# Queries and keys of all batches kept on chip, the forget gates' math in two groups, and half of a batch's rows normalised by the scalar engine

## The chip, the core and the metric

The kernel runs on one core of one Trainium2 chip. The core has a matrix engine (PE; PEld is its weight load), a vector engine (DVE), a scalar engine (ACT), GpSimd (POOL) and a sync engine (SP) that here only issues DMAs and waits. A name with a q (SPq, ACTq, POOLq) is the queue of DMAs that an engine issues. Each engine works through its own list of instructions in order; a semaphore wait holds everything behind it on that engine. The metric is the device time of one execution in microseconds (us).

## The reference

Two layers over x of 16 batches x 256 rows x 256 columns, all in float32:

```python
# layer 1: matrix-LSTM cross attention, queries from LN(x), keys and values from ctx
q = layernorm(x)                                   # (x - mean) / sqrt(var + eps)
i_gate = concat(q, ctx, ctx) @ igate_kernel + igate_bias     # 8 heads
f_gate = concat(q, ctx, ctx) @ fgate_kernel + fgate_bias
cs = cumsum(log_sigmoid(f_gate))                   # along the 256 rows
log_D = where(tril, cs_row - cs_col + i_gate_col, -inf)
m = max(log_D, -1);  D = exp(log_D - m)
C = (q @ k.T / sqrt(32)) * D                       # per head, 32 columns each
h = C / (max(|sum(C)|, exp(-m)) + 1e-6) @ v
x = x + head_layernorm(h) * outnorm_weight
# layer 2: mixture of 8 experts, top 2 per row
xn = layernorm(x)
y = sum over 2 best experts of p_e * w3_e (silu(w12_e xn)[:512] * (w12_e xn)[512:])
out = x + y
```

## The kernel before, in words

The program runs through four stages, one after the other on every engine.

**Stage 1, gates** (helper `gating`, `stage1` on each engine, 16 batches, b = 0 to 15). SP loads x (`X1`, L383) and the transposed context (`CT1`, L391). DVE takes mean and variance (L704, L708) and writes both halves of the normalised rows (`Q1`, L720). ACT turns the variance into 1/sqrt (Ln and Exp, L510, L512). PE's `turn` transposes `Q1` into a PSUM bank (four transposes, L1133); ACT copies that to `QT1` (L531), and SP stores it to the DRAM tensor `qT_scratch` (L386). PE's `gates` multiplies `QT1` and `CT1` by the gate kernels (eight matmuls, L1145 and L1147), ACT copies the 16 x 256 result to `GS1` (L537), SP stores that to `gate_scratch` (L396). The engines run this skewed: in step b of the loop DVE does the statistics of batch b and the rows of b-1; ACT does Ln and Exp of b, the copy of b-1, the gate copy of b-2; PE does `turn(b-1)` and then `gates(b-2)`. In every second step ACT also rounds a piece of the expert weights w12 to a high part (`high`, L517) and POOL subtracts it to get the low part (`low`, L1015); a piece is 128 x 512. w12 has 32 pieces; stage 1 does 8 of them, 8 more go between the stages and before, 16 in stage 2.

**Between the stages.** The gates of all 16 batches x 8 heads are read back as two 128 x 256 tiles (L405). ACT and DVE compute log-sigmoid, the two scans and the running maximum (L559 to L563, L735 to L743), ACT, POOL and DVE split two tiles into three bfloat16 parts (`parts`), ACT makes the decay factors `dcol` (L571 to L573), PE transposes them (L1160), DVE copies them to `cols` (L747). SP stores the parts to `g_scratch` and `negM_scratch` (L433, L435). SP also loads mask constants (L409, L412) and the first queries. Stage 2 waits for all of it.

**Stage 2, mixing** (`mixing`, `step(b, i)`). Per batch SP loads from DRAM the gate rows (`LG`, `RM`), the keys again (`KT`, L417), the queries spread by head (`QBD`, four DMAs, L419), the context with a column of ones (`AUG`, L463), the keys as rows (`KN`, L464) and half of the queries once more (`QTB`, L465). PE computes the exponents (L1177), scores (L1190), products with the values (L1208), the state of the first half of the rows (L1221; its input `VW` is made by POOL, L1054, from `AUG` and `cols`), its product with the queries (L1242) and the router's scores. ACT's Exp (L583) and DVE's product (L799, `combine`) stand between.

**Routing** (DVE: top 2, positions, one-hot tables, `hots`, L941 and L942) with PE's small matmuls; SP loads the eight w3 tensors meanwhile (L479). **Experts**: 71 tiles of 128 rows, gathered by POOL and added back to the output.

Of the kernel before, what the change touches and what calls it, by code (L numbers as in the profile page):

```python
# [34 lines left out]
P = 128  # L35
# [26 lines left out]
MROWS = GROWS + HALF + 1  # L62

# [20 lines left out]
def build(nc, x, ctx, ctxv, ctxT, gkq, gkk, gkv, ibias, fbias, onw, w12T, w3T, gateT, ident, lgc, rmc, trib, iota, iota16, codes, floors, spares, out):  # L84

    qT_dram = nc.dram_tensor("qT_scratch", (B, P, NG, S), F32).ap()
    gate_dram = nc.dram_tensor("gate_scratch", (B, 2 * NH, S), F32).ap()
# [11 lines left out]
    with ExitStack() as stack:  # L99
# [3 lines left out]
        def sem(name):  # L103
# [26 lines left out]
        KT = [sb(f"kt{i}", [P, NG, S], on=early) for i in range(2)]  # L130
# [15 lines left out]
        rs1 = [sb(f"rs1_{i}", [P, NC], on=a) for i in range(4)]  # L146
        parts = sb("parts", [P, 2, PARTS, S], BF16, on=a)
        rest = sb("rest", [P, 2, PARTS - 1, S], on=a)
        zeros = sb("zeros", [P, S], on=a)
        zrow = sb("zrow", [P, ROW], on=a)  # L150

        a1 = ExitStack()
        X1 = [sb(f"x1_{i}", [P, NC, E], on=a1) for i in range(4)]
        CT1 = [sb(f"ct1_{i}", [P, NK, S], on=a1) for i in range(4)]
        a1.close()

        gi, gf, fa, fm, fe, fl, lsg, cs, g, M, negM, mx = (
            sb(n, [P, S], on=a) for n in ("gi", "gf", "fa", "fm", "fe", "fl", "lsg", "cs", "g_", "M_",
                                          "negM", "mx"))
        dcol = sb("dcol", [P, 4, P], on=a)  # L160
        a.close()
# [3 lines left out]
        QTB = [sb(f"qtb{i}", [P, NG, P], on=m) for i in range(2)]  # L165
# [16 lines left out]
        m.close()  # L182
        early.close()
# [43 lines left out]
        def two(name):  # L227
# [6 lines left out]
        qT_out, gate_out = two("qT_out"), two("gate_out")  # L234
# [5 lines left out]
        pair_in, pair_dve, pair_act, m_parts, g_parts, g_there, g_rest, parts_out = sems(  # L240
            "pair_in", "pair_dve", "pair_act", "m_parts", "g_parts", "g_there", "g_rest", "parts_out")
        abs_ready, log_ready, g_ready, dcol_ready, cols_psum, cols_ready = sems(
            "abs_ready", "log_ready", "g_ready", "dcol_ready", "cols_psum", "cols_ready")
        wst_in = two("wst_in")
        pieces2_in = [sem(f"pieces2_in_{n}") for n in range(B // 2 - 2)]
        w_hi, w_lo = sems("w_hi", "w_lo")
# [23 lines left out]

        def gating(eng, step, peeled=4):


            for b in range(peeled):
                step(b, b % 4)
            with eng.Fori(peeled // 4, B // 4) as it:
                for x in range(4):
                    step(it * 4 + x, x)
            for b in range(B, B + 2):
                step(b, b % 4)  # L280
# [33 lines left out]
        def flat(t):  # L314
            return t[:].rearrange("p k s -> p (k s)")

# [3 lines left out]
        PIECES0, PIECES2 = (0, 2), tuple(range(4, B, 2))  # L320
        W0 = len(PIECES0)
        EARLY2 = 2
        W1 = W0 + B
        W2 = W1 + len(PIECES2)

        BUF2 = [flat(t) for t in (Q1[0], Q1[1], QT1[0], QT1[1])] + [t[:] for t in wst]
        IN0, IN1 = 16 * W0 // 2, 16 * (W0 + B // 2) // 2
        K1 = 2 * NC
        LOADS3 = 1 + HG + 3

        LOADSV = 3

        def load2(eng, n):

            at = PIECES2[n] * HID
            eng.dma_start(BUF2[n], w12T[:, at:at + HID]).then_inc(pieces2_in[n], 16)

# [17 lines left out]
        def _(sp):  # L355

            for b in range(2):
                sp.dma_start(X1[b][:], x_t[b]).then_inc(x1_in[b], 16)
            sp.dma_start(id_f[:], ident).then_inc(consts_in, 16)
            for dst, src in ((gq, gkq), (gk, gkk), (gv, gkv)):  # L360
                sp.dma_start(dst[:], src.rearrange("p (k g) -> p k g", k=NK)).then_inc(consts_in, 16)

# [14 lines left out]
            def stage1(b, x):  # L377

                old, o = b - 5, 1 - x % 2
                if has(b, 0) and (not isinstance(b, int) or b >= 2):  # L380

                    wait(sp, q_ready, b - 3)
                    sp.dma_start(X1[x][:], x_t[b]).then_inc(x1_in[x], 16)  # L383
                if has(b, 5):
                    sp.wait_ge(qT_ready, old + 1)
                    sp.dma_start(qT_dram[old], QT1[o][:]).then_inc(qT_out[o], 16)  # L386
                if has(b, 1):

                    y = (x + 3) % 4
                    wait(sp, gates_psum, b - 4)  # L390
                    sp.dma_start(CT1[y][:], ctxT_t[b - 1]).then_inc(ct1_in[y], 16)  # L391
                if isinstance(b, int) and b == 3:
                    later_constants()
                if has(b, 5):
                    sp.wait_ge(gates_ready, old + 1)
                    sp.dma_start(gate_dram[old], GS1[o][:]).then_inc(gate_out[o], 16)  # L396
            gating(sp, stage1, peeled=8)
            for b in range(B + 2, B + 5):
                stage1(b, b % 4)


            for i in range(2):
                sp.wait_ge(gate_out[i], 16 * (B // 2))
            for k, dst in enumerate((gi, gf)):
                sp.dma_start(dst[:], gate_dram[:, k * NH:(k + 1) * NH, :]).then_inc(pair_in, 16)  # L405

            for i in range(2):
# [7 lines left out]
            def load_scores(b, i):  # L415

                sp.dma_start(KT[i][:], ctxT_t[b]).then_inc(in3[i], 16)  # L417
                for j in range(HG):
                    sp.dma_start(QBD[i][j * DH:(j + 1) * DH, :, j, :],  # L419
                                 qT_dram[b, j * DH:(j + 1) * DH]).then_inc(in3[i], 16)  # L420

            for i in range(2):
                sp.wait_ge(qT_out[i], 16 * (B // 2))
            sp.wait_ge(zeroed, 1)
            load_scores(0, 0)

            sp.wait_ge(gates_psum, B)
            sp.wait_ge(w_lo, W1)
            for n in range(EARLY2, len(PIECES2)):
                load2(sp, n)  # L430
            for q in range(PARTS):
                sp.wait_ge(g_parts, q + 1)
                sp.dma_start(g_dram[:, q], parts[:, 1, q, :]).then_inc(parts_out, 16)  # L433
            sp.wait_ge(m_parts, 2 * PARTS - 1)
            sp.dma_start(negM_dram.rearrange("a q s -> q a s"), parts[:, 0]).then_inc(parts_out, 16)  # L435

            sp.wait_ge(parts_out, 16 * (1 + PARTS))
# [957 lines left out]
```

## Time and profile before

| | us |
|---|---|
| median of 3 runs | 681.81 (678.13 to 685.04) |
| the profiled execution | 680.75, span 679.0 |
| stage 1, first transpose to last gate copy | 11.4 to 62.4 |
| first state matmul of stage 2 | 88.4 |
| routing | about 260 to 311 |
| experts | 311 to 679 |
| granted TensorE clock, mean | 0.923 |

Busy time over the whole span, from the page: PE 565.5 us, DVE 465.2, ACT 331.7, POOL 305.3. These are averages over stages with different limits. A timeline row merges neighbouring instructions of one kind: where it starts, for how long, engine, line, what it writes and reads, and in brackets how long the engine was idle before and what ended that. A clock of 1.00 is the level of 2.4 GHz, 0.50 that of 1.2 GHz.

### The profile page before, as it was taken

Reading aid. Unit: us, or ns where it says so; the run is one execution under the profiler, and the core shown is the slowest. Engines: PE = TensorE matmul, PEld = TensorE weight load, DVE = VectorE, ACT = ScalarE, POOL = GpSimd, SP = SyncE. Lnnn points to the kernel's source line nnn. Section 1 sums busy time; section 2 is a strip of 40 time slices with the busy share of each in tenths; the row PEclk is TensorE's granted clock in tenths of the full one; section 3 lists DMA queues with packets and bytes.
Section 4 is the critical chain, followed back from the end, with each engine's and each line's share of the span. In section 5 each row is a group of like instructions: output and inputs, shape, how many; then the busy total and the mean of one; then the engine's idle time right before and its main releaser. Section 6 shows DMA issues by size and latency. Waiting matters only on the chain.

```text
span 679.0 us, 15003 instructions
## 1 busy us (share of the span) xinstructions
PE 565.5 (83%) x3608; PEld 465.6 (69%) x3609; DVE 465.2 (69%) x976; ACT 331.7 (49%) x736; POOL 305.3 (45%) x312
## 2 busy tenths in 40 slices
PE   3876098988988985124999999999999999999993
PEld 1332077877877864012888888888888888888883
DVE  3664336788878887993676767667677767676763
ACT  3444345566666753001555555555555555555551
POOL 2233325465655742002354545455555555454532
PEclk9999588999999995555999999999999999999998
DMA  9885575566666633601133333323333333333332
GB/s 284 251 297 187 173 203 159 175 210 209 200 202 220 192 113 110 255 4 44 33 56 56 50 60 48 62 47 63 47 59 52 55 55 54 55 52 58 48 47 24
DMA packets 72293, 77.51 MB, mean 114 GB/s; under 512 B 12930, under 2 KB 64266, under 8 KB 72268
## 3 DMA queue, kind: packets, MB, share of 16 engines
q0 software_dynamic: 15712, 25.73, 20.5%
q1 hardware_dynamic: 47564, 42.59, 20.4%
q10 hardware_dynamic: 8992, 8.92, 3.8%
q8 instruction: 9, 0.15, 0.1%
q14 instruction: 16, 0.13, 0.1%
HBM read 53.99 MB, written 23.21 MB: 114 GB/s over the span
## 4 chain that ended last, share of the span: by engine, by line
issue 42%; DVE 16%; POOL 12%; DMA 11%; PE 11%; SPq 4%; ACT 2%; DVEq 0%; ACTq 0%; POOLq 0%
POOL xg L1093 8%; DMA out_rows<-ys,index 6%; PE bank L1208 5%; POOL out_rows L1102 4%; DMA qT_scratch<-qt 4%; PE dots L1190 3%; DVE c L799 3%; DVE ohn L942 2%; DVE ohp L941 2%; DVE st L704 1%; DVE tot L838 1%; DVE mu L833 1%; DVE wden L834 1%; DMA gv<-in_gkv 1%; DVE mv L708 1%
## 5 line engine op out<-in xcount | busy, mean ns | idle before, releaser
L1102 POOL DMA_INDIRECT out_rows<-ys,index x71 | 112.9, 1590 | 155.7 <-DVE ys L994 149.3
L1000 DVE TENSOR_TENSOR w3l<-w,w3h 128x1024 fp32r<-128x1024 f32 x71 | 87.1, 1227 | 30.9 <-issue 29.9
L1093 POOL DMA_INDIRECT xg<-token_table,index x71 | 70.4, 991 | 74.7 <-DVE index L959 52.9
L671 ACT CAST w3h<-w 128x1024 fp32r x71 | 74.4, 1048 | 20.1 <-issue 20.1
L1208 PE MATMUL bank<-aug,c 128*128 128x99 f32 (+2 forms) x512 | 65.2, 282 | 15.5 <-DVE c L799 15.3
L1322 PE MATMUL bank<-w3l,hth 128*128 128x256 f32 x284 | 76.5, 302 | 1.7 <-DVE w3l L1000 1.7
L1208 PEld LDWEIGHTS bank<-aug,c 128*128 128x128 f32 x512 | 61.2, 196 | 22.4 <-DVE c L799 19.9
L1323 PE MATMUL bank<-w3h,hth 128*128 128x256 f32 x284 | 70.8, 282 | 0.0
L977 DVE TENSOR_TENSOR htl<-bank,hth 128x512 fp32r<-128x512 f32 x71 | 49.1, 691 | 25.2 <-ACT hth L661 25.2
L994 DVE TENSOR_SCALAR ys<-bank,pc 128x256 f32<-128x256 f32 x71 | 34.4, 484 | 46.5 <-PE bank L1326 46.5
L1294 PE MATMUL weighs<-w12l,xh 128*128 x144 | 62.2, 432 | 1.1 <-DVE xl L966 1.1
L666 ACT CAST xh<-bank 128x256 fp32r<-128x256 f32 x70 | 26.1, 373 | 68.3 <-PE bank L1281 68.3
L1294 PE MATMUL dots<-w12l,xh 128*128 x140 | 58.3, 416 | 1.0 <-DVE xl L966 1.0
L1296 PE MATMUL weighs<-w12h,xh 128*128 x144 | 57.7, 400 | 0.0
L1295 PE MATMUL weighs<-w12h,xl 128*128 x144 | 57.6, 400 | 0.0
L1296 PE MATMUL dots<-w12h,xh 128*128 x140 | 55.2, 394 | 0.0
L1322 PEld LDWEIGHTS bank<-w3l,hth 128*128 128x128 f32 x284 | 53.8, 189 | 2.0 <-issue 2.0
L1295 PE MATMUL dots<-w12h,xl 128*128 x140 | 55.1, 394 | 0.0
L1323 PEld LDWEIGHTS bank<-w3h,hth 128*128 128x128 f32 x284 | 54.1, 191 | 0.0
L1015 POOL TENSOR_TENSOR w12l<-wst,w12h 128x512 f32 (+1 forms) x28 | 35.5, 1271 | 40.7 <-ACT w12h L517 40.4
L799 DVE SCALAR_TENSOR_TENSOR c<-dots,d 128x512 f32<-128x512 f32 x64 | 41.2, 685 | 18.0 <-PE dots L1190 17.3
L1326 PE MATMUL bank<-w3h,htl 128*128 128x256 f32 x284 | 45.6, 283 | 0.0
(169 smaller groups left out, 1221.6 us busy)
## 6 DMA issues: line engine op xcount, KB each, us to landing
x<-in_x SPq DMA_DIRECT2D x32, 256.0 KB, 3.3
wst<-in_w12T POOLq DMA_DIRECT2D x26, 256.0 KB, 3.7
aug<-in_ctxv SPq DMA_DIRECT2D x16, 264.0 KB, 3.6
ct<-in_ctxT SPq DMA_DIRECT2D x16, 256.0 KB, 4.8
qT_scratch<-qt SPq DMA_DIRECT2D x16, 256.0 KB, 3.7
kt<-in_ctxT SPq DMA_DIRECT2D x16, 256.0 KB
qbd<-qT_scratch SPq DMA_DIRECT2D x64, 64.0 KB
out_rows<-x ACTq DMA_DIRECT2D x16, 256.0 KB, 2.2
```

What stands on the lines that cost most here:

```text
L671: nc.scalar.copy(W3H[i][:], w3[:, bass.ds(e, 1)].rearrange("p a k d -> p (a k d)")).then_inc(w3h_ready, 1)
L799: v.scalar_tensor_tensor(C[:, r_, :], dots[:, r_, :], KS, D[:, r_, :], ALU.mult, ALU.mult).then_inc(c_ready, 1)
L977: v.tensor_tensor(HTL[o][:].rearrange("p k s -> p (k s)"), bank[5][:], HTH[o][:].bitcast(F32).rearrange("p k s -> p (k s)"), ALU.subtract) ...
L1000: v.tensor_tensor(W3L[i][:], w3[:, bass.ds(e, 1)].rearrange("p a k d -> p (a k d)"), W3H[i][:].bitcast(F32), ALU.subtract).then_inc(w3l_re ...
L1093: q.indirect_dma_start(out=XG[x][:], out_offset=None, in_=table, in_offset=bass.IndirectOffsetOnAxis(ap=index[:, j:j + 1], axis=0)).then_i ...
L1102: q.indirect_dma_start(out=out, out_offset=bass.IndirectOffsetOnAxis(ap=index[:, j:j + 1], axis=0), in_=YS[o][:], in_offset=None, compute_ ...
L1208: ins = mm(bank[4 + c][:, h * DV:h * DV + wide], C[:, j // 2, from_:from_ + P], AUG[i][:].rearrange("p c h d -> p (c h d)")[:, at:at + wid ...
L1294: mm(acc, XH[i][:, k, :], wl, start=(k == 0), stop=False)
L1295: mm(acc, XL[i][:, k, :], wh, start=False, stop=False)
L1296: ins = mm(acc, XH[i][:, k, :], wh, start=False, stop=(k == NK - 1))
L1322: mm(acc, HTH[o][:, k, :], W3L[o][:, k * E:(k + 1) * E], start=(k == 0), stop=False)
L1323: mm(acc, HTH[o][:, k, :], W3H[o][:, k * E:(k + 1) * E], start=False, stop=False)
```

## The change

Queries and keys no longer go through DRAM. The tensors `w12h` and `w12l` hold 32 pieces each; the last 16 pieces' places hold, until that piece's weights are written in stage 2, the transposed queries (in `w12h`) and keys (in `w12l`) of one batch each. The `KT` and `QTB` loads go; `QBD` is filled by DMAs from SBUF. The first 8 pieces are loaded in stage 1, pieces 16 to 31 in stage 2, pieces 8 to 15 after stage 2, while routing runs. The places of pieces 8 to 15 serve stage 1 and the gate math as buffers. The gate rows go by DMA straight into the tiles `gi` and `gf`. The gate math runs twice: for 4 batches (partitions 96 to 127) inside stage 1, for the other 12 (partitions 0 to 95) in steps 0 to 3 of stage 2. Of each batch, DVE normalises the first 128 rows, ACT the second 128. The clearing of `QBD` and `KVB` moves from DVE to POOL and to the start.

```diff
+LEAD = 4
+AHEAD = slice(P - LEAD * NH, P)
+REST = slice(0, P - LEAD * NH)
+KEPT = PIECES - B          # 16
...
+        def room(flat_, at, width):
+            return flat_[:, at * HID:at * HID + width].bitcast(F32)
+        def kept(flat_, b):
+            return flat_[:, bass.ds((b + KEPT) * HID, HID)].bitcast(F32).rearrange("p (k s) -> p k s", k=NK)
...  SP, stage 1
+            for b in range(B + 5):
+                old = b - 5
+                if 2 <= b < B:
+                    wait(sp, q_ready, b - 3)
+                    wait(sp, q1_ready, b - 3)
+                    sp.dma_start(X1[b % 4], x_t[b]).then_inc(x1_in[b % 4], 16)
+                if 1 <= b <= B:
+                    wait(sp, gates_psum, b - 4)
+                    sp.dma_start(kept(flat_l, b - 1), ctxT_t[b - 1]).then_inc(ct1_in[(b - 1) % 4], 16)
+                if b in (9, 11):
+                    mask_constants((b - 9) // 2)
+                if 0 <= old:
+                    sp.wait_ge(gates_ready, old + 1)
+                    at = (old - LEAD) % B * NH
+                    for k, dst in enumerate((gi, gf)):
+                        sp.dma_start(dst[at:at + NH, :], GS1[old % 2][k * NH:(k + 1) * NH, :]
+                                     ).then_inc(gate_out[old % 2], 16)
+                if b == B:
+                    pair_rows(0)
+                    sp.wait_ge(zeroed, 1)
+                    load_queries(0, 0)
+                if b == B + 1:
+                    sp.wait_ge(parts_out, 16 * (1 + PARTS))
+                    load_gates(0, 0)
...  SP, stage 2
                     sp.dma_start(KN[i][:], ctx_t[b, :, 0, :]).then_inc(inv3[i], 16)
-                    sp.dma_start(QTB[i][:], qT_dram[b, :, :, P:S]).then_inc(inv3[i], 16)
+                if isinstance(b, int) and b == LEAD - 1:
+                    pair_rows(1)
+                    sp.wait_ge(parts_out, 32 * (1 + PARTS))
...
+            for n in range(KEPT // 2):
+                at = (KEPT // 2 + n) * HID
+                sp.dma_start(room(flat_l, KEPT // 2 + n, HID), w12T[:, at:at + HID]).then_inc(late_in[n], 16)
+            sp.wait_ge(w_lo, W2)
...  ACT, stage 1
                 if has(b, 1):
+                    a_, y = b - 1, (x - 1) % 4
+                    act.wait_ge(nb1_ready, a_ + 1)
+                    nc.scalar.activation(Q1[o][:, 1, :], X1[y][:, 1, :], ACT.Identity, bias=nb1[y][:, 0:1],
+                                         scale=rs1[y][:, 1:2]).then_inc(q1_ready, 1)
                     act.wait_ge(qT_psum, a_ + 1)
-                    nc.scalar.copy(QT1[o][:]...
+                    nc.scalar.copy(kept(flat_h, a_)...
...
+            for b in range(B + 2):
+                stage1(b, b % 4)
+                if b == 8:
+                    act.wait_ge(late_consts, 16 * N_LATE)
+                    forget(0)                      # Abs, Exp, Ln on 32 partitions
+                if b == 11:
+                    gate_parts(0, 0, 2)            # each waits for g_rest from POOL
+                    decays(0)                      # three Exp into dcol
+                if b == 12:
+                    gate_parts(0, 2, 3)
...  ACT, stage 2
+                if isinstance(b, int) and b == 0:
+                    forget(1)
+                if isinstance(b, int) and b == 1:
+                    gate_parts(1, 0, 2)
+                    decays(1)
+                    gate_parts(1, 2, 3)
...
+            for n in range(KEPT // 2):
+                high(KEPT // 2 + n, room(flat_l, KEPT // 2 + n, HID), 16, late_in[n])
...  DVE, stage 1
-                    for c in range(NC):
-                        ins = v.tensor_scalar(Q1[o][:, c, :], X1[y][:, c, :], ...)
+                    v.scalar_tensor_tensor(nb1[y][:], mv1[y][:, 1, 0:1], -1.0, rs1[y][:, 1:2], ...)
+                    v.tensor_scalar(Q1[o][:, 0, :], X1[y][:, 0, :], ...)
...
+            for b in range(B + 1):
+                stage1(b, b % 4)
+                if b == 8:
+                    preactivation(0)               # waits for ACT's Ln; then lsg, scan cs, g
+                if b == 10:
+                    maxima(0)
+                if b == 11:
+                    three_parts(dve, v, negM, AHEAD, m_parts, 0)
+                if b == 14:
+                    columns(0, bank[4])
...  DVE, stage 2
                 def combine(c):
+                    if c == 1 and isinstance(b, int) and b == 1:
+                        preactivation(1)
+                        maxima(1)
...
+                if isinstance(b, int) and b == 2:
+                    columns(1, bank[7])
...
+                if isinstance(b, int) and b == 1:
+                    three_parts(dve, v, negM, REST, m_parts, 2 * PARTS - 1)
...  POOL
+            for b in range(B + 2):
+                if b % 2:
+                    n = (b - 1) // 2
+                    if n < W1:
+                        load_w(n, n % 2, n - 1)
+                    if n >= 1:
+                        low(n - 1, wst[(n - 1) % 2][:], n)
+                if b == 12:
+                    pool.wait_ge(w_lo, 5)
+                    gate_rests(0)
...
+            for n in range(KEPT // 2):             # after stage 2
+                low(KEPT // 2 + n, room(flat_l, KEPT // 2 + n, HID), W2 + n + 1)
...  PE
             def turn(b, i):
                 pe.wait_ge(q_ready, b + 1)
+                pe.wait_ge(q1_ready, b + 1)
                 wait(pe, qT_ready, b - 1)
...
+            for b in range(B + 2):
+                stage1(b, b % 4)                   # turn(b - 1), then gates(b - 2)
+                if b == 13:
+                    columns(0, bank[4])
...
             pe.wait_ge(tables, 1)
+            pe.wait_ge(w_lo, PIECES)
```

## Rows read from the trace of the kernel before

**Rows 1.** Busy time by stretch: PE, PEld, DVE, ACT, POOL, granted clock, DMA share, GB/s.

```profile
11.40:57.40 46.00, 38.23 (x172) 17.19 (x172) 28.41 (x87) 21.14 (x62) 10.83 (x12) 1.00 0.87 275
...
88.40:260.00 171.60, 153.40 (x1180) 130.19 (x1180) 132.78 (x291) 106.00 (x274) 94.05 (x137) 0.96 0.60 187
260.00:311.00 51.00, 13.64 (x90) 9.14 (x90) 45.98 (x211) 4.90 (x13) 0.00 (x0) 0.50 0.32 108
```

**Rows 2.** Waits between 0 and 64 us: total, times, longest.

```profile
ACT qt L531 <- DMA qT_scratch<-qt: 16.9, 13, 2.8
```

**Rows 3.** Timeline at the end of stage 1, at the high clock: start, duration.

```profile
55.05 0.66 PE L1133 MATMUL weighs<-id_f,q 128*128 128x128 f32 x4 [0.49 <-DVE q L720]
...
57.47 0.66 PE L1133 MATMUL weighs<-id_f,q 128*128 128x128 f32 x4
57.58 0.36 ACT L537 COPY gs<-dots 16x256 f32<-16x256 f32 x1 [0.91 <-PE dots L1147]
...
62.04 0.36 ACT L537 COPY gs<-dots 16x256 f32<-16x256 f32 x1 [1.69 <-PE dots L1147]
```

**Rows 4.** Timeline of the first batches, at the lower speed of the matmuls.

```profile
12.96 1.12 PE L1133 MATMUL weighs<-id_f,q 128*128 128x128 f32 x4 [0.50 <-DVE q L720]
...
17.64 0.36 ACT L537 COPY gs<-dots 16x256 f32<-16x256 f32 x1 [2.94 <-PE dots L1147]
```

**Rows 5.** Timeline of ACT: a rounding; and gate copy to Exp without one.

```profile
27.46 0.61 ACT L517 CAST w12h<-wst 128x512 f32 x1
...
54.90 0.36 ACT L537 COPY gs<-dots 16x256 f32<-16x256 f32 x1
...
55.49 0.20 ACT L512 ACTIVATE rs<-lnv 128x2 f32<-128x2 f32 x1
```

**Rows 6.** Groups by line, 120 to 240 us: busy, mean ns, idle before.

```profile
L631 ACT ACTIVATE x2n<-x,nb,rs 128x256 f32<-128x256 f32 x22 | 11.9, 586 | 0.0
```

**Rows 7.** A gap of PE in stage 1 (timeline), and two short stretches (columns as in rows 1).

```profile
37.73 1.04 PE L1145 MATMUL dots<-qt,gq 128*16 128x256 f32 x4 [1.22 <-ACT qt L531]
...
112.00:114.00 2.00, 0.13 (x2) 0.00 (x0) 1.85 (x6) 0.79 (x3) 0.00 (x0) 1.00 0.18 50
114.00:116.00 2.00, 1.74 (x8) 1.74 (x9) 1.05 (x4) 1.82 (x6) 0.42 (x1) 0.51 0.54 165
```

**Rows 8.** Timeline of the gate math between the stages.

```profile
68.59 0.51 ACT L559 ACTIVATE fa<-gf,fb 128x256 f32<-128x256 f32 x1 [2.38 <-DMA gf<-gate_scratch]
...
70.10 0.42 DVE L737 TENSOR_TENSOR lsg<-fm,fl 128x256 f32<-128x256 f32 x1 [1.09 <-ACT fl L563]
...
71.91 0.41 ACT L569 CAST parts<-g_ 128x256 bf16<-128x256 f32 x1 [1.91 <-POOLq L1041]
...
73.10 0.40 ACT L569 CAST parts<-rest 128x256 bf16<-128x256 f32 x1 [0.79 <-POOL rest L1045]
...
75.35 0.40 ACT L573 ACTIVATE dcol<-mx 128x256 f32<-128x256 f32 x1
```

**Rows 9.** Timeline of the start of stage 2.

```profile
84.08 0.47 SPq L464 DMA_DIRECT2D kn<-in_ctx  x1
...
88.43 1.25 PE L1221 MATMUL bank<-vw,kn 128*128 128x132 f32 x4 [0.30 <-POOL vw L1054]
```

**Rows 10.** Timeline: DVE beside POOL and without it (stage 1), the statistics of a batch.

```profile
24.24 0.86 DVE L720 TENSOR_SCALAR q<-x,mv,rs 128x256 f32<-128x256 f32 x2
...
26.98 0.25 DVE L708 BATCH_NORM_AGGREGATE mv<-st 128x2 f32<-128x6 f32 x2 [0.15 <-DVE st L704]
...
28.29 1.26 POOL L1015 TENSOR_TENSOR w12l<-wst,w12h 128x512 f32 x1 [4.18 <-ACT w12h L517]
...
28.54 1.48 DVE L720 TENSOR_SCALAR q<-x,mv,rs 128x256 f32<-128x256 f32 x2 [1.31 <-ACT rs L512]
```

**Rows 11.** Groups by line, 258 to 312 us; and a timeline row of SP's queue.

```profile
L942 DVE TENSOR_SCALAR ohn<-io,jf,code 128x72 f16<-128x72 bf16 x64 | 19.0, 297 | 0.0
...
273.89 3.94 SPq L479 DMA_DIRECT2D w<-in_w3T  x8
```

More of the change, by code:

```diff
@@ L355, in _ @@
         def _(sp):
[L357 to L358 removed]
+            sp.dma_start(X1[0], x_t[0]).then_inc(x1_in[0], 16)
             sp.dma_start(id_f[:], ident).then_inc(consts_in, 16)
@@ L375, in later_constants, with mask_constants @@
                     sp.dma_start(out[at:at + P, :], zrow[:, 0:E]).then_inc(zero_out, 16)
[L377 to L407, printed above, removed]
+            def mask_constants(i):
                 for lo, hi in ((0, PARTS), (GROWS, MROWS - 1), (MROWS - 1, MROWS)):
@@ L427, in _ @@
[L427 to L437, printed above, removed]
@@ new lines, in forget @@
+            def forget(part):
+                rows_ = (AHEAD, REST)[part]
+                for i in range(2):
+                    act.wait_ge(gate_out[i], 16 * (LEAD, B)[part])
+                nc.scalar.activation(fa[rows_, :], gf[rows_, :], ACT.Abs, bias=fb[rows_, 0:1]).then_inc(abs_ready, 1)
+                act.wait_ge(abs_ready, part + 1)
+                nc.scalar.activation(fe[rows_, :], fa[rows_, :], ACT.Exp, scale=-1.0).then_inc(pair_act, 1)
+                act.wait_ge(pair_act, part + 1)
+                nc.scalar.activation(fl[rows_, :], fe[rows_, :], ACT.Ln, bias=1.0).then_inc(log_ready, 1)
@@ new lines, in gate_parts, with decays @@
+            def gate_parts(part, lo, hi):
+                rows_ = (AHEAD, REST)[part]
+                for q in range(lo, hi):
+                    act.wait_ge(g_rest, PARTS * part + q + 1)
+                    src = g[rows_, :] if q == 0 else rest[rows_, 1, q - 1, :]
+                    nc.scalar.copy(parts[rows_, 1, q, :], src).then_inc(g_parts, 1)
+            def decays(part):
+                rows_ = (AHEAD, REST)[part]
+                act.wait_ge(g_ready, part + 1)
+                act.wait_ge(dcol_zero, 1)
+                nc.scalar.activation(dcol[rows_, 0, :], g[rows_, 0:P], ACT.Exp, bias=negM[rows_, P - 1:P])
+                nc.scalar.activation(dcol[rows_, 1, :], negM[rows_, P:S], ACT.Exp, bias=M[rows_, P - 1:P])
+                nc.scalar.activation(dcol[rows_, 2:4, :].rearrange("p a s -> p (a s)"), mx[rows_, :], ACT.Exp,
+                                     scale=-1.0).then_inc(dcol_ready, 1)
@@ L558, in _ @@
-            act.wait_ge(pair_in, 32)
-            nc.scalar.activation(fa[:], gf[:], ACT.Abs, bias=fb[:, 0:1]).then_inc(abs_ready, 1)
-            act.wait_ge(abs_ready, 1)
-            nc.scalar.activation(fe[:], fa[:], ACT.Exp, scale=-1.0).then_inc(pair_act, 1)
-            act.wait_ge(pair_act, 1)
-            nc.scalar.activation(fl[:], fe[:], ACT.Ln, bias=1.0).then_inc(log_ready, 1)
-            for q in range(PARTS):
-                act.wait_ge(g_rest, q + 1)
-                src = g[:] if q == 0 else rest[:, 1, q - 1, :]
-                nc.scalar.copy(parts[:, 1, q, :], src).then_inc(g_parts, 1)
@@ L1232, in step @@
                     ins.then_inc(x2t_psum, 1)
+                if isinstance(b, int) and b == 2:
+                    pe.wait_ge(o1_taken, 2)
+                    columns(1, bank[7])
                 if main:
@@ L1258, in step @@
                     values(b, i, 1)
+            pe.wait_ge(qT_ready, B)
             exponents(0, 0, 0)
-            mixing(pe, step)
+            pe.wait_ge(gates_ready, B)
+            for b in range(B + 3):
+                step(b, b % 2)
             pe.wait_ge(r_ones, 1)
```

298 lines of the change are left out of this document (136 added, 162 removed).

## The prediction, as written before the result was known

> **What bounds the kernel now.** I read the table by stretch first, to see what limits each stage. In stage 1 the DMA engines move 275 GB/s at a share of 0.87, and no compute engine but PE (38.2 of 46 us) is near full; in stage 2 PE has 153.4 of 171.6 us; in routing DVE has 46.0 of 51 us and POOL nothing; the experts are not touched [rows 1]. Then the waits of stage 1: ACT's copy waited 16.9 us for stores of transposed queries [rows 2]. These stores are what the change removes. Between the last gate copy at 62.0 us [rows 3] and the first state matmul at 88.4 us [rows 9] PE does almost nothing: that is the gate math, stores and loads. So the change attacks two real costs, the stores and the gap. What it puts in their place I worked out from the order of the code, engine by engine, with durations from the timeline. Batches came every (57.47 - 11.37) / 15 = 3.07 us before: the last `turn` began at 57.47 [rows 3], the first at 11.37 (the first timeline number of the table).
>
> **The new ring in stage 1.** ACT's step b is now: Ln and Exp of b, the identity for half of batch b-1, wait for `turn(b-1)`, its copy, wait for `gates(b-2)`, gate copy of b-2, in odd steps a rounding. PE's step is `turn(b-1)`, then `gates(b-2)`. PE can't start `turn(b)` before ACT's identity of b; ACT reaches that identity only after the gate copy of b-2; that copy needs `gates(b-2)`, which PE does after `turn(b-1)`. Before, DVE made the rows and ran one step ahead, so PE had its next transposes waiting. Now nothing of PE's work overlaps ACT's chain. One turn of the ring at the high clock:
> - `turn` start to gate copy start: 57.58 - 55.05 = 2.53 us [rows 3];
> - gate copy start to the end of Exp: 55.49 + 0.20 - 54.90 = 0.79, and 0.51 more with a rounding (0.61 less the overlap of 0.1 between ACT's instructions) [rows 5];
> - the identity, 0.59 for 128x256 [rows 6], less 0.1 of overlap, plus 0.05 for the semaphore: 0.53.
>
> That is 3.85 us, with a rounding 4.36; seven of 15 have one: 15 turns take 61.3 us. At the low clock `turn` to gate copy is 17.64 - 12.96 = 4.68 [rows 4], so 6.00 and 6.51: 93.6 us. The statistics, DVE's half and the DMAs fit beside either: without query stores a batch moves about 0.65 MB, 2.4 us at 275 GB/s. I cost them at nothing; uncovered, the period could not be above 3.85 through them.
>
> **The clock** decides between the two. Before, PE's gaps in stage 1 were up to 1.22 us and the clock stayed at 1.00 (2.4 GHz); after a gap in which PE did 0.13 of 2 us it was granted 0.51 (1.2 GHz) [rows 7]. In the ring PE waits 1.3 us in even turns, 1.8 in odd ones, and over 4 us at each stall below. So I take 7 of 15 turns at the low level: the first two, two after each stall, one more. 8 x 4.09 + 7 x 6.24 = 76.4 us. Ends: 61.3 and 93.6.
>
> **Stalls of group 0 in stage 1.** The operations run on 32 partitions; nothing shows such forms of the scans, so between 0 and the 128-partition time; I take the latter, since the time of these rows goes with the 256 columns. At step 8: Abs, Exp, Ln, 70.10 - 68.59 = 1.5 us on ACT; DVE, which waits for them inside its step, then does three operations in 71.91 - 70.10 = 1.8 [rows 8] and only then the statistics of batch 9, 1.15 us (0.15 and 0.25 of the aggregates [rows 10], behind two operations over 256 columns of 0.42 each by the first DVE row of [rows 8], less 0.1 of overlap). ACT's next Ln waits for these: 4.4 us. At steps 11 and 12: ACT's copy waits for POOL, whose `low` of the piece just rounded comes first, 1.3 [rows 10]; then from the first copy to the last Exp 75.75 - 71.91 = 3.8 [rows 8], less 0.8 as the third copy no longer waits for POOL: 4.3. Maxima and parts on DVE hide beside the ring, which leaves DVE over 1.5 us a turn. Together 8.7, low end 4.
>
> **From the last `turn` to the first state matmul.** 62.04 - 57.47 = 4.6 to the last gate copy [rows 3], 0.4 for it. SP waits for that copy before it issues two gate rows (0.35 each) and the loads of `AUG` and `KN` of batch 0; those now stand behind it. From the issue of `KN` to the matmul it was 88.43 - 84.08 = 4.35 [rows 9], less 0.5 for the `QTB` issue that is gone. With 0.45 for the issue of `AUG`: 10.0 us, where it was 88.43 - 57.47 = 31.0. So 21.0 are won here.
>
> First state matmul: 11.4 + 76.4 + 8.7 + 10.0 = 106.5, against 88.4: **+18.1**.
>
> **Stage 2.** `KT` and `QTB` loads go. PE is busy for nine tenths [rows 1] and isn't ended by them in the rows; 0 taken, at best -2. Addresses that are computed per batch for keys and queries: 0, at worst +3. Group 1 adds on ACT the 1.5 and the 4.3 less POOL's `low` 1.3, on DVE before `combine(1)` of step 1 the 1.8 and about as much for the three of `maxima`, then 2 for the parts, and PE's four transposes. ACT and DVE overlap in part, and PE stands behind both: 3.6 + 2 + 1.4 = **+7**, ends 3 and 12 (a clock drop with it).
>
> **The late pieces.** Pieces 8 to 15 are loaded, rounded and subtracted in routing. POOL was idle there [rows 1], DVE full. A DVE operation with one input in SBUF lasted 1.48 us (for two) beside POOL's subtraction of 1.26 us, and 0.86 without it [rows 10]: it stood still. Routing's tables are 64 pairs of such operations [rows 11]. Eight subtractions, 8 x 1.27 = 10.2 us, back to back, issued from where the w3 loads started, 273.9 [rows 11]. A tenth of DVE's work there reads PSUM: **+9**, ends 0 and 10. The w3 loads end some 5 us later, hidden up to 311.
>
> Sum: 18.1 + 7 + 9 = 34.1; the profiled execution took 680.75 (its span and 1.75 around), so **715 us**. It lies 1.1 below the median of the runs, which I leave inside the range.
>
> A rule to weigh: the Trainium skill, "Perfetto Trace Analysis", section "Optimizing Scalar/DVE Operations", says that offloading from DVE to ACT may make sense if DVE is saturated. In stage 1 DVE is busy 28.4 of 46 us [rows 1]. The rule's condition fails here, so it speaks against this part. Were DVE the limit, 16 halves of 0.43 us, 7 us, would be won; the ring costs more.
>
> **Rivals.**
> 1. *The ring, high clock nearly throughout.* For: the gap of 1.22 us that did no harm [rows 7]. Then 61.3: 91.4 at the first state matmul, +3.0 +7 +9: 700; with group 1 at its low end and half of the late pieces' cost 691. Chance 0.23.
> 2. *The ring at the low level throughout.* For: the longer gaps. 93.6, and 2 more at the end: 734. Chance 0.12.
> 3. *The ring, but stalls, group 1 and late pieces mostly covered.* 61.3 with stalls of 4, then +3 and +0: 680.75 - 1.7 + 3 + 0 = 682. Against: DVE full in routing. Chance 0.08.
> 4. *The stores were the bound and nothing takes their place: faster.* The place is the period of a batch: if ACT's identity were ready in time, PE alone needs 57.47 - 55.05 = 2.42 us [rows 3]; 36.3 for 15, first state matmul at 66.4, -22.0 + 7 + 9: 675, with low ends 662. With the other terms as taken it decides below a period of (61.3 - 19) / 15 = 2.8 us, since 61.3 gives +19. Against: the order of the waits in the code. Chance 0.10.
>
> **Numbers.** The forecast of 715, from 702 to 724, has 0.47. The range 690 to 735 takes in nearly all of rivals 1 and 2, 0.8 together, and leaves out 3 and 4. Within 1% (6.8 us, about what a measurement can tell from no change): 3 and the upper end of 4, 0.10. Faster by over 1%: the rest of 4, 0.08. Slower: 0.82.
>
> **What would show it.** Ring: in stage 1 every group of four transposes ends its idle time on ACT's identity, ACT's gate copy starts 1.9 us after `gates` starts, and transposes follow each other by 3.9 to 6.5 us. Stalls: a PE gap over 4 us at steps 9 and 12. Start of stage 2: the state matmul 10 us after the last `turn`. Late pieces: DVE's table operations of over 1 us while POOL subtracts. I am wrong if transposes come every 3 us or less, or if POOL and DVE run side by side in routing.

## The result, and the profile after

| | before | after |
|---|---|---|
| median of 4 runs each, us | 680.81 (678.13 to 685.04) | 704.53 (702.46 to 708.66) |
| ratio, 95% interval | | 1.0366 [1.033, 1.0403] |
| profiled execution; span | 680.75; 679.0 | 702.92; 701.2 |
| moved by DMA, MB | 77.51 | 66.87 |
| first `turn` | 11.37 | 8.50 |
| last `turn` | 57.47 | 89.98 |
| first state matmul | 88.43 | 99.84 |
| last state matmul | 244.19 | 260.43 |
| `abf`, the start of the routing tables | 274.30 | 290.24 |
| `index`, their end | 310.81 | 333.06 |

The kernel became 3.7% slower; the prediction of 715 us, range 690 to 735, lies 10.5 above the median. The span grew by 22.2 us. Read off the table: +11.4 up to the first state matmul, +4.8 to the last (155.8 before, 160.6 after), -0.3 to `abf`, +6.3 to `index`, and nothing in the experts (368.2 and 368.1).

Busy time of the kernel after by stretch, columns as in [rows 1]: all turns of stage 1; stage 2; the part of routing in which the late pieces are subtracted.

```profile
8.50:90.00 81.50, 47.69 (x177) 19.96 (x177) 27.50 (x100) 34.30 (x88) 12.71 (x15) 0.83 0.47 142
...
99.84:260.43 160.59, 145.30 (x1108) 123.97 (x1108) 124.67 (x277) 101.99 (x264) 86.40 (x127) 0.95 0.51 154
...
290.24:304.00 13.76, 0.61 (x2) 0.13 (x2) 12.47 (x28) 4.94 (x8) 10.38 (x8) 0.50 0.95 343
```

The stores that held up ACT [rows 2] are gone from the list of waits. The DMA share of stage 1 fell from 0.87 [rows 1] to 0.47, but mostly because the stage is longer: from these rows I estimate 12.7 MB before (275 GB/s for 46.0 us) and 11.6 MB after (142 GB/s for 81.5 us). The 15 turns take 81.5 us instead of 46.1, and no engine is near full. That is what a ring of waits looks like: everybody is idle in turn. Three of the longest waits between 0 and 110 us:

```profile
...
ACT gs L521 <- PE dots L1188: 29.9, 16, 2.9
DVE nb L722 <- ACT rs L496: 28.8, 9, 6.9
...
PE weighs L1174 <- DVE w12h L724: 19.7, 7, 6.0
```

ACT waits for PE's gates in each of 16 batches, DVE and PE for what ACT does next. One turn of the ring in the timeline, the part that answers to [rows 3] and [rows 5]:

```profile
27.76 0.63 PE L1174 MATMUL weighs<-id_f,w12h 128*128 128x128 f32 x4 [1.42 <-DVE w12h L724]
...
28.32 1.04 PE L1186 MATMUL dots<-w12h,gq 128*16 128x256 f32 x4
...
30.25 0.36 ACT L521 COPY gs<-dots 16x256 f32<-16x256 f32 x1 [1.25 <-PE dots L1188]
30.52 0.61 ACT L501 CAST w12h<-wst 128x512 fp32r<-128x512 f32 x1
...
31.47 0.58 ACT L512 ACTIVATE w12h<-w12h,nb,rs 128x256 f32<-128x256 f32 x1
...
32.16 0.63 PE L1174 MATMUL weighs<-id_f,w12h 128*128 128x128 f32 x4 [1.94 <-issue]
```

ACT's identity (L512) ends at 32.05, and the transposes start at 32.16. The gate copy starts 1.93 us after the gates. Step with a rounding: 32.16 - 27.76 = 4.40 us. At steps 9 and 12 stand the two stalls:

```profile
41.82 0.63 PE L1174 MATMUL weighs<-id_f,w12h 128*128 128x128 f32 x4 [1.94 <-issue]
44.32 0.36 ACT L521 COPY gs<-dots 16x256 f32<-16x256 f32 x1 [1.24 <-PE dots L1188]
44.70 0.50 ACT L531 ACTIVATE w12l<-w12l,fb 32x256 f32<-32x256 f32 x1
46.20 0.42 DVE L740 TENSOR_TENSOR w12l<-w12l 32x256 f32<-32x256 f32 x1 [8.46 <-ACT w12l L535]
...
49.19 0.29 ACT L494 ACTIVATE lnv<-mv,eps 128x2 f32<-128x2 f32 x1 [3.09 <-DVE mv L711]
50.31 1.09 PE L1174 MATMUL weighs<-id_f,w12h 128*128 128x128 f32 x4 [6.03 <-DVE w12h L724]
...
70.14 1.08 PE L1174 MATMUL weighs<-id_f,w12h 128*128 128x128 f32 x4 [5.98 <-DVE w12h L724]
...
99.84 1.25 PE L1266 MATMUL bank<-vw,kn 128*128 128x132 f32 x4 [4.08 <-POOL vw L1087]
```

And in routing, where POOL was idle before, DVE's instructions beside POOL's eight subtractions:

```profile
293.31 10.38 POOL L1048 TENSOR_TENSOR w12l<-w12l,w12h 128x512 fp32r<-128x512 f32 x8 [19.30 <-ACT w12h L501]
294.89 1.37 DVE L959 TENSOR_TENSOR ta<-oh,slotS 128x256 f32<-128x256 f32 x1
...
298.88 1.19 DVE L962 TENSOR_SCALAR sj<-sloti 128x64 int32<-128x64 int32 x1
300.00 1.30 DVE L963 TENSOR_SCALAR sp_<-sloti 128x64 int32<-128x64 int32 x1
...
303.77 0.25 DVE L974 TENSOR_SCALAR ohp<-io,pf 128x128 f16<-128x128 bf16 x1
```

The first one-hot table comes 13.5 us after `abf`; before it was 7.2 (281.52 - 274.30).

### The profile page after: what moved, and what is told of

Read it like the earlier page. It is cut to its first block, busy times and chain, and to the rows that moved or that the text cites. A ratio compares the mean times of both kernels' runs of the same rounds, so it can differ in the third digit from the quotient of the medians.

```text
span 701.2 us, 14675 instructions
## 1 busy us (share of the span) xinstructions
PE 574.4 (82%) x3612; PEld 470.1 (67%) x3613; DVE 465.9 (66%) x987; ACT 344.5 (49%) x761; POOL 309.9 (44%) x316
## 2 busy tenths in 40 slices
DMA packets 61148, 66.87 MB, mean 95 GB/s; under 512 B 12146, under 2 KB 55034, under 8 KB 61116
## 4 chain that ended last, share of the span: by engine, by line
issue 42%; DVE 18%; PE 15%; POOL 12%; DMA 7%; ACT 2%; SPq 2%; DVEq 0%; POOLq 0%; ACTq 0%
POOL xg L1133 8%; DMA out_rows<-ys,index 5%; PE bank L1253 5%; POOL out_rows L1142 4%; PE dots L1235 3%; PE dots L1186 3%; DVE c L828 2%; PE dots L1188 2%; DVE ohn L975 2%; DVE tot L869 2%; DVE ohp L974 1%; DVE st L707 1%; DVE mu L864 1%; PE weighs L1174 1%; DVE wden L865 1%
## 5 line engine op out<-in xcount | busy, mean ns | idle before, releaser
L1253 PE MATMUL bank<-aug,c 128*128 128x99 f32 (+2 forms) x512 | 67.7, 288 | 16.5 <-DVE c L828 16.5
L1253 PEld LDWEIGHTS bank<-aug,c 128*128 128x128 f32 x512 | 63.6, 202 | 23.0 <-DVE c L828 21.2
L1048 POOL TENSOR_TENSOR w12l<-wst,w12h 128x512 fp32r<-128x512 f32 (+1 forms) x24 | 30.5, 1270 | 74.8 <-ACT w12h L501 74.6
L1174 PE MATMUL weighs<-id_f,w12h 128*128 128x128 f32 x64 | 11.9, 317 | 42.3 <-DVE w12h L724 19.7
```

The source lines that it names most:

```text
L1253: ins = mm(bank[4 + c][:, h * DV:h * DV + wide], C[:, j // 2, from_:from_ + P], AUG[i][:].rearrange("p c h d -> p (c h d)")[:, at:at + wid ...
```

## The experiments

Each ratio is against the kernel before, run on the same chip. "After" is 1.0366 by that measure. The ratios are the safer comparison between experiments; the times come from several chips, and a profile shows one execution.

**e1_dve_both.** The kernel after, but DVE normalises both halves.

```diff
  ACT  -  nc.scalar.activation(Q1[o][:, 1, :], X1[y][:, 1, :], ACT.Identity, ...)
  DVE  +  v.tensor_scalar(Q1[o][:, 1, :], X1[y][:, 1, :], ...).then_inc(q1_ready, 1)
```

> The changed kernel with DVE normalising both halves again, everything else as changed. Theory of the ring (ACT's identity must wait for the gate copy, that for gates, that for turn): without the identity on ACT, DVE has the rows ready a step ahead, transposes follow each other by 2.4 to 2.9 us instead of 4.4 to 5.6, the clock stays at 1.00 between the stalls, and first to last turn takes about 50 us instead of 81.5; time about 673 us. Rival, the stalls of the gate math and the slower clock alone are the price: the same 8.5 us steps remain and DVE has 7 us more to do, time 698 to 706 us.

680.97 us, ratio 1.0031 [1.0005, 1.0056]. The state matmul is at 77.22, 22.6 earlier than in the kernel after. So ACT's half of the normalisation, which closes the ring, costs the 23 us, and everything else in the change adds up to about nothing: the state matmul comes 11.2 us earlier than in the kernel before (88.43), and stage 2 (161.4 us instead of 155.8) and `abf` to `index` (42.8 instead of 36.5) give that back. It is not the 673 us that I expected of the ring theory. The turns take 57.2 us (8.02 to 65.23) and 10.2 of them are one step:

```profile
21.65 0.66 PE L1171 MATMUL weighs<-id_f,w12h 128*128 128x128 f32 x4
24.07 0.66 PE L1171 MATMUL weighs<-id_f,w12h 128*128 128x128 f32 x4
...
34.68 0.36 ACT L518 COPY gs<-dots 16x256 f32<-16x256 f32 x1 [3.39 <-DMA w12l<-gs]
36.56 0.42 DVE L737 TENSOR_TENSOR w12l<-w12l 32x256 f32<-32x256 f32 x1 [6.24 <-ACT w12l L532]
40.24 1.09 PE L1171 MATMUL weighs<-id_f,w12h 128*128 128x128 f32 x4 [7.74 <-DVE w12h L719]
```

Without the ring transposes follow each other by 2.42 us where nothing else stands in the way. In the long step DVE stood in its program order before group 0's math, which waited 6.24 us for ACT's Ln, and ACT stood 3.39 us before a buffer whose DMAs were queued on SP behind the mask constants.

**e2_gates_first.** The kernel after with PE's two calls exchanged, so that ACT's gate copy no longer waits for the newest `turn`.

```diff
  PE   +  if has(b, 2): gates(b - 2, (x - 2) % 4)
          if has(b, 1): turn(b - 1, 1 - x % 2)
       -  if has(b, 2): gates(b - 2, (x - 2) % 4)
```

> The changed kernel with only PE's order in a step of stage 1 turned round: gates(b-2), then turn(b-1). No work added or taken from any engine. Ring theory: PE's gates now run beside ACT's Ln, Exp and identity; the period becomes gates 1.9 + turn 0.6 + copy 0.6 and semaphores, about 3.3 us, at the high clock; first to last turn about 58 us with the stalls, time about 682 us. Rival, ACT simply has too much work per batch: nothing changes, 702 to 706 us.

688.14 us, ratio 1.0136 [1.0084, 1.0188]. ACT does all it did before, and the steps fall to 3.16 us:

```profile
20.07 0.66 PE L1174 MATMUL weighs<-id_f,w12h 128*128 128x128 f32 x4
23.23 0.66 PE L1174 MATMUL weighs<-id_f,w12h 128*128 128x128 f32 x4
...
39.88 0.63 PE L1174 MATMUL weighs<-id_f,w12h 128*128 128x128 f32 x4 [3.93 <-DVE w12h L724]
```

So the order of the waits was the cost, not ACT's load. The state matmul comes at 79.78, 20.1 us earlier than in the kernel after and only 2.6 behind e1: of what the ring cost there, the exchange gives back nearly nine tenths. Of these 20.1 us 4.6 are lost again in stage 2, whose code is untouched: it takes 165.2 us in this profile and 160.6 in the kernel after, and PE is busy for 31.3 of its first 40 us instead of 35.7. Why is not shown. Together with the turns, 61.7 us instead of the expected 58, this covers the 6 us by which the expectation was missed. In the turns each `gates` now stands directly behind ACT's copy of the queries (0.68 us idle in each step), and the stalls stay (7.2 us at 32.72 to 39.88).

**e3_before_act_half.** The kernel before with only the halves shared out.

```diff
  ACT  +  act.wait_ge(nb1_ready, a_ + 1)
       +  nc.scalar.activation(Q1[o][:, 1, :], X1[y][:, 1, :], ACT.Identity, ...)
  DVE  -  for c in range(NC): v.tensor_scalar(Q1[o][:, c, :], ...)
       +  v.scalar_tensor_tensor(nb1...);  v.tensor_scalar(Q1[o][:, 0, :], ...)
  PE   +  pe.wait_ge(q1_ready, b + 1)
```

> The kernel before with one part of the change alone: ACT normalises the second 128 rows of each batch. Ring theory: the ring arises here too, 3.9 to 4.4 us per batch at the high clock, more at the low one, instead of 3.07; 15 us to 28 us slower than before, 696 to 709 us. Rival, the half on ACT is harmless and the damage is in the other parts: within 3 us of before.

705.18 us, ratio 1.0401 [1.0335, 1.0467]. The split alone, with the old stores still in place, costs all of the loss. In its profiled execution, the fastest of the four, the span is 20.0 us longer than before and the turns take 67.7 us instead of 46.1. Its steps carry the idle times of the ring:

```profile
33.16 0.63 PE L1140 MATMUL weighs<-id_f,q 128*128 128x128 f32 x4 [1.94 <-issue]
37.04 0.63 PE L1140 MATMUL weighs<-id_f,q 128*128 128x128 f32 x4 [1.42 <-issue]
```

PE waits 1.42 and 1.94 us by turns, as in the kernel after, and these two turns are 3.88 us apart.

**e4_small_late_low.** The kernel after, with POOL's late subtractions on 8 of 512 columns; the low parts of pieces 8 to 15 are left out except for these columns.

```diff
  POOL -  low(KEPT // 2 + n, room(flat_l, KEPT // 2 + n, HID), W2 + n + 1)
       +  q.tensor_tensor(flat_l[:, at:at + 8], ..., ALU.subtract)
```

> The changed kernel with POOL's eight subtractions after stage 2 done on 8 of 512 columns each; the low part of the other columns of these eight pieces of w12 is left out. Theory that POOL holds DVE up in routing: DVE's operations of 0.7 to 1.4 us return to 0.2 to 0.4, 6.4 us less, about 698 us. Rival, the loads or ACT's roundings do it: no more than 1 us less.

698.67 us, ratio 1.0305 [1.0242, 1.0367], 5.9 below the kernel after by the medians and 4 by the ratios, whose intervals overlap; the profile is what shows the effect. From `abf` (290.41) to the first one-hot table (297.65) it is 7.24 us again:

```profile
294.93 0.43 DVE L959 TENSOR_TENSOR ta<-oh,slotS 128x256 f32<-128x256 f32 x1
...
296.98 0.20 DVE L962 TENSOR_SCALAR sj<-sloti 128x64 int32<-128x64 int32 x1
```

0.43 and 0.20 us where the kernel after needed 1.37 and 1.19. The loads and ACT's roundings are still there, so they are not the cause. The late subtractions cost 6.3 us of DVE's time, all of it before the one-hot tables.

**e8_group0_later.** The kernel after with DVE's part of group 0 one step later.

```diff
  DVE  -  if b == 8: preactivation(0)
       +  if b == 9: preactivation(0)
```

> The changed kernel as it is, with only DVE's part of group 0 one step later, after the statistics of batch 9. The ring is untouched. Theory that the statistics stood behind a wait for ACT: the 8.5 us between the transposes of batches 7 and 8 becomes 5.5 to 6, 2 to 3 us less than the changed kernel. Rival: ACT waits for DVE anyway, 0.

701.95 us, ratio 1.0317 [1.0276, 1.0358], 2.6 below the kernel after; the intervals touch. The step of the first stall is 6.92 us instead of 8.49, where I expected 5.5 to 6; the second stall stays at 8.43. So DVE's order makes up 1.6 of the 4.6 us that this step has over a normal one of 3.89. What makes up the rest was not tested.

**e5_repaired.** e1, and: `preactivation(0)` at step 9; mask constants at steps 12 and 14; ACT's three parts at steps 11, 12 and 13, POOL's `gate_rests` in step 11 ahead of its subtraction; `AUG` and `KN` of batch 0 loaded during stage 1.

```diff
  SP   -  if b in (9, 11): mask_constants((b - 9) // 2)
       +  if b in (12, 14): mask_constants((b - 12) // 2)
       +  if b == B + 1: ... AUG[0], KN[0] loaded
  ACT  +  b == 11: gate_parts(0, 0, 1);  b == 12: gate_parts(0, 1, 2), decays(0);  b == 13: gate_parts(0, 2, 3)
```

> The changed kernel with DVE normalising both halves (as in the first experiment, about 681 us) and its four other waits of stage 1 taken away: DVE's part of group 0 one step later, the mask constants' loads at steps 12 and 14 instead of 9 and 11, the parts of the gates spread over ACT's steps 11 to 13, AUG and KN of batch 0 loaded before the last gate copies are stored. Theory that stage 1 is then bound by PE with short stalls: the 10 us step at batch 8 shrinks to under 5, that at batch 11 from 5 to 3, the state matmul follows the last turn by 8 instead of 12 us; about 670 us. Rival, the stalls only move to the next wait: 678 to 682 us.

670.96 us, ratio 0.9887 [0.9833, 0.9942]: 1.1% below the kernel before, a small difference whose interval is clear of 1. The two longest stalled steps shrank from 10.2 and 5.0 us in e1 to 5.4 and 3.7. The state matmul follows the last turn by 11.6 us, not by the 8 that I expected, so that the time of about 670 came out is in part luck. Several waits were taken away at once, and what each was worth is not separated. By stretch: the turns; to the first state matmul; stage 2; routing tables; experts.

```profile
8.03:54.88 46.85, 37.20 (x177) 17.21 (x177) 31.01 (x100) 25.22 (x71) 12.19 (x14) 1.00 0.78 243
54.88:66.47 11.59, 6.89 (x33) 3.40 (x32) 0.34 (x1) 3.56 (x8) 3.17 (x4) 0.82 0.28 74
66.47:229.38 162.91, 148.46 (x1109) 126.37 (x1109) 125.45 (x279) 101.89 (x264) 86.37 (x127) 0.93 0.50 153
259.19:301.94 42.75, 7.36 (x66) 4.14 (x66) 40.69 (x170) 5.17 (x9) 10.37 (x8) 0.50 0.45 151
```

Up to the first state matmul it wins 22.0 us over the kernel before. Hardly any of that is a shorter batch: the turns take 46.9 us (before 46.1). 19.4 us are won between the last turn and the state matmul (31.0 before), where the gate math no longer stands alone, and 3.3 by the earlier first turn. Stage 2 gives back 7.1 (162.9 against 155.8) and the late pieces 6.2 (42.75 against 36.5): 679.0 - 22.0 + 7.1 + 6.2 = 670.3, and the span is 669.5. So of the change's idea 22 us are real, and 13 of them are paid later.

**e6_late_in_tail.** e5 with the eight late pieces in steps 14 to 18 of stage 2, whose tail has no other pieces.

```diff
  all  +  LATE = {14: (0, 1), 15: (2, 3), 16: (4, 5), 17: (6,), 18: (7,)}
  SP, ACT, POOL: load, high, low of these pieces in step b (POOL: b + 1), not after stage 2
```

> The repaired kernel, with the eight late pieces loaded, rounded and subtracted in steps 14 to 18 of stage 2 (two each in 14, 15, 16, one each in 17 and 18) instead of in routing. Theory: POOL is idle for much of these steps and DVE waits for others there, so most of the 6.4 us comes back: 4 us less than the repaired kernel. Rival, POOL holds DVE up there just as much, or ACT's roundings lengthen the chain: within 1 us of it.

672.25 us, ratio 0.9874 [0.9831, 0.9918]: no gain over e5. Routing is back at 36.5 us (266.67 to 303.17), but from the last state matmul (230.14) to `abf` it is 36.5 instead of 29.8 (229.38 to 259.19). The waits of that tail, first of e5, then of e6:

```profile
PE bank L1277 <- ACT x2n L625: 5.4, 3, 3.9
...
ACT x2n L607 <- DVEq L872: 3.6, 2, 2.2
```

```profile
PE bank L1283 <- ACT x2n L627: 6.1, 2, 5.5
...
ACT x2n L609 <- DVEq L875: 6.0, 2, 3.0
...
PE bank L1261 <- DVE c L833: 3.4, 1, 3.4
```

The tail is a chain over ACT, DVE and PE; work put into it moves its end. One bill was exchanged for another. Whether it is POOL beside DVE or ACT's roundings that lengthen the chain is not separated.

**e7_maxima_later.** e5 with `maxima(1)` out of `combine(1)` of step 1, at the end of that step.

```diff
  DVE  -  preactivation(1); maxima(1)     (in combine(1), b == 1)
       +  preactivation(1)
       +  if b == 1: maxima(1); three_parts(...)     (end of the step)
```

> The repaired kernel, with the three operations of maxima for group 1 moved from before combine(1) of step 1 to the end of that step. Theory: PE's gap of 2.6 us before the values of step 1 shrinks below 1.5 us, the clock stays at 1.00, 3 to 5 us less than the repaired kernel. Rival, DVE is behind all the same: within 1 us.

669.81 us, ratio 0.9855 [0.9808, 0.9902], not to be told from e5. PE's gap shrank as expected, from 2.55 to 1.28 us:

```profile
85.52 1.97 PE L1255 MATMUL bank<-aug,c 128*128 128x99 f32 x16 [1.28 <-DVE c L829]
```

Stage 2 shrank from 162.9 to 159.7 us (68.55 to 228.22), but started 2.1 later, which the edit can't cause, since it stands behind that point. The next two kernels are a second such pair: 163.4 and 161.3 us, the second 3.1 later. Both differences are within the spread of kernels whose stage 2 is the same (159.9 to 165.2 us, see below), so what the edit is worth stays open.

**e9_late_after_slots** and **e10_maxima_and_late.** e5 and e7, in which POOL starts the late subtractions only when DVE has made its first pair of one-hot tables.

```diff
  POOL +  pool.wait_ge(hots_ready, 1)
          for n in range(KEPT // 2): low(...)
```

> The repaired kernel (DVE normalises both halves, group 0 placed in gaps) with one wait more on POOL: its eight late subtractions start when DVE's first pair of one-hot tables is done, not as soon as the late pieces are rounded. Theory (POOL's two-input subtractions hold up only DVE's instructions with two inputs and its int32 and cast ones, in the stretch from abf to the first one-hot table): that stretch goes back from 13.5 us to 7.2, the one-hot tables (bf16 in, f16 out, 0.25 and 0.30 us) run on beside POOL at one each 0.37 us, and the time is 6 us below the repaired kernel's 671.0, about 665. Rival (POOL's subtractions block the one-hot tables as well, as they block one another on the shared access): the first table starts 6 us earlier but the 64 pairs take up to 10 us more, index is not earlier, 671 to 675. Second rival: the w3 loads, which wait for POOL's last subtraction, come 11 us later and are now late: they landed about 282 and are first used near 317, so no loss is expected from them.

> The same wait on POOL, and group 1's maxima moved to the end of step 1. If both are worth what they were alone or are expected to be (1 us and 6 us): about 664, 1 us below the kernel with the wait alone, which this measurement may not tell. If the maxima's place only moved the wait, the same as the kernel with the wait alone.

e9: 676.87 us, ratio 0.997 [0.9953, 0.9987]. e10: 671.63, ratio 0.9903 [0.9882, 0.9924]. My theory, that the 16-bit tables run on beside POOL, fell. DVE in e9:

```profile
267.86 0.24 DVE L976 TENSOR_SCALAR ohp<-io,pf 128x128 f16<-128x128 bf16 x1
268.02 1.31 DVE L977 TENSOR_SCALAR ohn<-io,jf,code 128x72 f16<-128x72 bf16 x1
269.25 1.31 DVE L976 TENSOR_SCALAR ohp<-io,pf 128x128 f16<-128x128 bf16 x1
...
276.57 1.31 DVE L976 TENSOR_SCALAR ohp<-io,pf 128x128 f16<-128x128 bf16 x1
277.81 0.29 DVE L977 TENSOR_SCALAR ohn<-io,jf,code 128x72 f16<-128x72 bf16 x1
```

Exactly eight DVE instructions last 1.3 instead of 0.2 to 0.3 us, one for each of POOL's eight. From `abf` to `index` it is 44.8 us, 2.1 more than in e5 (the medians differ by 5.9; e9's profile is of its fastest execution of twelve, so what the rest is isn't shown). The wait made it worse: in e5 some of POOL's time ran beside DVE instructions that aren't held up. The profiled spans (672.3 and 672.0) don't show the 5 us between the medians of e9 and e10, so that difference stays open.

## Why the prediction was right, step by step

**The ring: right in mechanism and in time per turn.** High clock: 4.40 us with a rounding, 3.89 and 3.98 without; predicted 4.36 and 3.85. It was shown from three sides: taken out (e1, -23 us), its order changed with ACT's load kept (e2, -16), put alone into the kernel before (e3, +4.0%). One of my signs was wrong: the profile names ACT's identity only in the first 2 of 16 turns as what ended PE's idle time; it gives DVE's half or "issue", and only the times (identity ends 0.11 before the transposes) tell who was last. For this step I had taken 0.05 us, which no row gave.

**The clock: right that both levels occur, the size too high.** I took 7 of 15 turns at the low level, 6.24 us each. The clock's mean was 0.83 between 8.5 and 90 us, about a third of the time at the low level; to this come the first 8 us, for which the profile gives 1.00 although the transposes last 1.08 us, as they do at the low level. Besides the first turn and the two stalls, 7 steps had a low part. My count was nearly right, two after each stall among them, but these steps took 5.3 to 6.3 us, as only part of each was at the low level. The first took 3.52; PE had no gates to do in it yet. All turns took 81.5 us, stalls included; predicted 76.4 + 8.7 = 85.1.

**The stalls: right in size, in part in cause.** 8.49 us, where a step without a rounding takes 3.89, and 8.43, where one with a rounding takes 4.40: 4.6 and 4.0; predicted 4.4 and 4.3. Part of both steps was at the low level, and e8 took away only 1.6 us of the first, so the agreement is better than my account of it.

**The start of stage 2: right.** 99.84 - 89.98 = 9.86 us; predicted 10.0.

**The first turn: a term that was missing.** I let it stand at 11.4. It came at 8.50, since the gate kernels' constants land earlier (DVE waited 2.8 us for them, before 6.5). SP issues them 0.5 us earlier, and POOL's first loads of weights start at 4.86 instead of 1.49, behind the clearing that the change moved to it; which of the two does it was not tested. With 3.6 from the turns this is the difference between +18.1 and the +11.4 measured.

**Stage 2: +4.8, predicted +7.** The +4.8 is one profile. The five kernels that have this stage 2 unchanged took 159.9 to 165.2 us (the kernel after, e1, e2, e4, e8), so +4.1 to +9.5; e3, which has the old one, took 155.7, and the kernel before 155.8. I had put the weight on queues behind group 1's math. PE was held up once, 2.56 us:

```profile
117.36 1.28 DVE L828 SCALAR_TENSOR_TENSOR c<-dots,d 128x512 f32<-128x512 f32 x2
118.69 3.63 PE L1253 MATMUL bank<-aug,c 128*128 128x99 f32 x16 [2.56 <-DVE c L828]
```

Before that PE was busy for 15.7 of 16.3 us, at a mean clock of 0.85; over the first 40 us the clock was 0.81 (before 0.89). The steps between state matmuls are 10.7, 13.7, 11.8 and 10.3 us (before 9.1, 8.9, 13.3 and 9.6), then 10.4 (before 10.4 to 10.7). How the +4.8 divides between clock and group 1 was not separated.

**The late pieces: +6.3, predicted +9.** Right that POOL's subtractions hold up DVE (e4), wrong in which instructions: I had the one-hot tables held up, and the subtractions (293.31 to 303.69) ended just before the first of them (303.77). The cost was less because only part of DVE's instructions in that stretch are held up. e9 put the subtractions beside the tables, as I had pictured it, and there the cost rose to 8.3 (44.8 - 36.5), near my 9.

**The sum** was 12 us too high: 34.1 against 22.2. 2.9 of it is the first turn, 3.6 the turns, 2.2 stage 2, 2.7 the late pieces, the rest roundings and the tail. All of them have one sign, as I took the pessimistic value where a row left a choice. So the loss was overstated by half; that the median still lies well inside the range owes much to the range's width of 45 us.

Rival 4 (675, the stores were the bound and nothing takes their place) put the first state matmul at 66.4, and e5 has it at 66.47. The parts agree less well: 8.0 for the first turn (11.4), 46.9 for the turns with their stalls (36.3 + 8.7 = 45.0), 11.6 for the start (10.0). That the stores set the period before is shown only in part: where e5 has no group math, from 15.31 to 31.32, a batch takes 2.67 us, against 3.06 in the kernel before (17.53 to 35.86), and the steps with group 0's math use that up.

## What to carry to other kernels

Before moving work to a less busy engine, write down the order of every engine's step and look for a closed chain; half a batch's normalisation (0.43 us of DVE), moved to an ACT that was busy for less than half of the stage, cost 23 us over 16 batches, because ACT's previous task waited for PE's newest. Where such work is wanted, break the ring: as e2 shows, exchanging two calls on PE gives back 16 of the 23 us. Deferred work has its bill in the stretch where it lands, so cost that stretch too. For work of POOL on SBUF tensors look which instructions of DVE stand beside it: the reductions and those with one input in PSUM were not held up here. A stretch in which DVE often waits is not free by that alone: e6 tried one and gained nothing.

## What the runs showed of the hardware

**POOL holds up DVE one instruction at a time.** While POOL's 128x512 subtractions run back to back, 1.22 to 1.3 us each, DVE gets in one instruction of certain kinds per subtraction, whatever its own length: int32 on 64 columns 0.20 to 1.19, f16 from bf16 0.25 to 1.31. A product with both inputs in SBUF went from 0.43 to 1.37. A TENSOR_REDUCE did not (0.42 in both), nor did a difference with one input in PSUM (`weighs`, 0.42 in both). The rows of e5, with POOL busy from 262.20 to 272.57:

```profile
262.33 0.42 DVE L956 TENSOR_TENSOR slotS<-cum,weighs 128x256 f32<-128x256 f32 x1
...
263.78 1.37 DVE L961 TENSOR_TENSOR ta<-oh,slotS 128x256 f32<-128x256 f32 x1
265.18 0.42 DVE L962 TENSOR_REDUCE slot<-ta 128x32 f32<-128x256 f32 x1
```

The Trainium skill, "SBUF — State Buffer", section "Who interferes with whom", says that the two engines share a pair of ports as an exclusive lock, that `tensor_scalar`, copies and casts can take it as well as `tensor_tensor` with two inputs in SBUF, and that `tensor_reduce` never contends. All of these rows agree; my expectation for e9 went against that rule and was wrong.

**The clock can fall without a long gap.** In the ring PE's gaps were 1.42 and 1.94 us, and the granted clock of short stretches without a stall was still below 1.00, so part of them was at the low level (17 to 28 us and 28 to 42 us):

```profile
17.00:28.00 11.00, 6.83 (x26) 2.79 (x27) 4.53 (x19) 4.89 (x13) 1.81 (x2) 0.84 0.45 134
28.00:42.00 14.00, 8.69 (x38) 3.54 (x37) 3.56 (x13) 6.56 (x17) 2.93 (x3) 0.88 0.49 139
```

In e5, with PE busy 37.2 of 46.9 us, it was 1.00 throughout the turns, in spite of one gap of 2.95 us. Only the first two groups of transposes, at 8.03 and 11.57, took 1.08 us, as at the low level, while the profile gives 1.00 there too; so at the start of a trace the length of a known matmul is the better guide than the clock in the row.
